# A three-stage hybrid layer: first tiles, router, gathers and weights of each stage fetched and prepared inside the stage before it

## The reference, cut to what matters

```
x = x + attn_a(layernorm(x))     # softmax attention, 16 heads of 64, rotary q and k, full (not causal)
x = x + ffn(layernorm(x))        # one expert of 8 per sequence, chosen from the sequence's last row
x = x + attn_b(layernorm(x))     # causal linear attention in buckets of 64
x = x + ffn(layernorm(x))        # the same weights again

def ffn(h):                      # h: [B, S, 1024]
    last = h[:, -1, :]
    logits = gelu(last @ Wp1 + bp1) @ Wp2 + bp2       # the router, in fp32
    sel = argmax(softmax(logits), -1)
    w1, w2 = W1[sel], W2[sel]                         # [1024, 2048] and [2048, 1024] per sequence
    t = gelu(h @ w1 + b1[sel]) @ w2 + b2[sel]
    return h + 0.3 * (t @ Wo + bo)

def attn_b(h):                   # q, k, v = h @ Wq.T, h @ Wk.T, h @ Wv.T, in 16 heads
    q = softmax(q * 64**-0.25, -1); k = elu(k * 64**-0.25) + 1
    context = cumsum(k.T @ v over buckets) / (cumsum(sum of k) + 1e-6), shifted by one bucket
    return (q @ context) @ Wo.T + bo
```

## Time and profile before

| | |
|---|---|
| median of 3 runs | 3585.08 us |
| the profiled execution | 3589.35 us |
| its span, slowest core (4) | 3587.6 us |
| spans of the eight cores | 3550.1 to 3587.6 us |
| mean granted TensorE clock of the cores | 0.946 to 0.953 |
| TensorE busy | 3156.5 us (88%), 16026 instructions |
| ScalarE, VectorE, POOL busy | 1766.9, 1426.8, 720.7 us |
| chain that ended last, by engine | PE 67%, DVE 8%, ACT 7%, DMA 7%, issue 6%, POOL 4% |

### The profile page before, as it was taken

How to read it: one execution, slowest core, us unless ns; L and a number is a source line. 1 busy time by engine, 2 the same in 40 slices (tenths; PEclk the granted TensorE clock), 3 DMA queues, 4 the chain that set the end, 5 groups by cost and what they waited for, 6 DMA issues and landing times.

```text
span 3587.6 us, 48068 instructions; the slowest of 8 cores (3550.1 to 3587.6 us)
## 1 busy us (share of the span) xinstructions
PE 3156.5 (88%) x16026; PEld 1291.3 (36%) x16026; DVE 1426.8 (40%) x2150; ACT 1766.9 (49%) x2011; POOL 720.7 (20%) x834
## 2 busy tenths in 40 slices
PE   3899999985899999983899899689999946999999
PEld 1332222222332222221344344245545522444444
DVE  3545555543545555432122122156656640232122
ACT  3339999973259999951232223145544422222221
POOL 3410000002310000003321312123322214123311
PEclk9999999997999999995999899899999977999999
DMA  9100000114100001117611421441111129123211
GB/s 169 57 1 1 15 34 25 35 44 119 41 1 1 24 26 35 36 54 146 129 48 48 94 76 43 109 85 60 60 66 64 44 84 158 58 84 70 73 47 48
DMA packets 74892, 216.04 MB, mean 60 GB/s; under 512 B 12128, under 2 KB 14240, under 8 KB 74272
## 3 DMA queue, kind: packets, MB, share of 16 engines
q1 hardware_dynamic: 49728, 157.87, 13.4%
q0 software_dynamic: 24928, 55.11, 9.8%
HBM read 198.80 MB, written 69.21 MB: 75 GB/s over the span
## 4 chain that ended last, share of the span: by engine, by line
PE 67%; DVE 8%; ACT 7%; DMA 7%; issue 6%; POOL 4%; SPq 0%; DVEq 0%; ACTq 0%; POOLq 0%
PE wide L791 12%; PE wide L780 10%; PE bank L683 10%; PE wide L673 6%; PE wide L822 6%; ACT e_sb L1250 6%; PE bank L806 6%; PE bank L910 3%; PE bank L650 3%; PE bank L698 3%; PE bank L689 3%; DMA w2s<-fW,idxw 2%; PE bank L581 2%; PE wide L606 1%; DVE pv_x L1000 1%
## 5 line engine op out<-in xcount | busy, mean ns | idle before, releaser
L1250 ACT ACTIVATE e_sb<-wide 128x1024 bf16<-128x1024 f32 x1024 | 1019.5, 1027 | 86.2 <-PE bank L683 37.4
L683 PE MATMUL bank<-e_sb,v_sb 128*128 128x512 bf16 x2048 | 620.5, 381 | 13.3 <-DVE pv_x L1000 10.1
L780 PE MATMUL wide<-f_xnT,w1s 128*128 128x512 bf16 x2048 | 458.3, 385 | 80.1 <-DMA w1s<-fW,idxw 49.1
L791 PE MATMUL wide<-h_sb,w2s 128*128 128x512 bf16 x2048 | 464.4, 384 | 24.5 <-issue 12.8
L1274 ACT ACTIVATE h_sb<-wide,b1f 128x512 bf16<-128x512 f32 x256 | 175.7, 687 | 550.3 <-PE wide L780 481.9
L673 PE MATMUL wide<-ring,k_sb 64*128 64x512 bf16 x2048 | 401.7, 388 | 16.6 <-ACT e_sb L1250 11.2
L383 POOL TENSOR_TENSOR rt<-raw,cos_t 128x512 bf16<-128x512 bf16 x128 | 147.7, 1154 | 1001.9 <-DVE raw L1038 778.4
L780 PEld LDWEIGHTS wide<-f_xnT,w1s 128*128 128x128 bf16 x2048 | 202.1, 99 | 333.5 <-issue 99.2
L1085 DVE COPY f_xnT<-bank 128x1024 bf16<-128x1024 bf16 x64 | 44.1, 691 | 682.7 <-PE bank L581 682.7
L791 PEld LDWEIGHTS wide<-h_sb,w2s 128*128 128x128 bf16 x2048 | 199.7, 98 | 268.0 <-issue 42.2
L673 PEld LDWEIGHTS wide<-ring,k_sb 64*128 64x128 bf16 x2048 | 103.0, 93 | 443.8 <-issue 443.8
(11 more groups left out here) (175 smaller groups left out, 3559.8 us busy)
## 6 DMA issues: line engine op xcount, KB each, us to landing
a_xt<-xin SPq DMA_DIRECT2D x64, 512.0 KB, 3.8
f_xt<-xs SPq DMA_DIRECT2D x64, 512.0 KB, 4.2
xs<-a_xt SPq DMA_DIRECT2D x32, 512.0 KB, 2.7
xs<-f_xt SPq DMA_DIRECT2D x32, 512.0 KB, 4.9
b_xt<-xs SPq DMA_DIRECT2D x32, 512.0 KB, 3.3
xs<-b_xt SPq DMA_DIRECT2D x32, 512.0 KB, 2.6
yout<-f_xt SPq DMA_DIRECT2D x32, 512.0 KB, 4.5
wof<-fWo POOLq DMA_DIRECT2D x4, 1024.0 KB, 18.4
```

The source lines that it names most:

```text
L683: ins = t.matmul(half[4 + hh], v_sb[:, kc, hp, hh * 64:hh * 64 + 128], e_sb[:, i % 4, hh * 512:(hh + 1) * 512], start=(kc == 0), stop=(kc ...
L780: ins = t.matmul(half[fc % 2], w1s[s][:, c, fc * 128:(fc + 1) * 128], xT[:, c, :], start=(c == 0), stop=(c == NCH - 1))
L791: ins = t.matmul(half[2 + jc % 2], w2s[:, fc, jc * 128:(jc + 1) * 128], h_sb[:, fc, :], start=(fc == 0), stop=(fc == NFC - 1))
L1250: a.activation(e_sb[:, i % 4, :], wide[i % 2][:].rearrange("p a b -> p (a b)"), AF.Exp, scale=INV_SCALE_A).then_inc(sm["ex"], N("ex", (s, i)))
```

## The change: what it does, and the diff

- `all_of` is gone. Engines wait for the single results that they need.
- SBUF is laid out by offsets (`put`), stage by stage, so that what a stage fetches early lies where the stage before has already finished. `w2s` becomes two halves of eight chunks in separate places; it is still one copy of w2.
- Start: four tile buffers (`x_buf`: `a_xt` and `a_xe`) instead of two for sequence 0.
- Sequence 1 of stage 0: tiles 0 to 7 are loaded, normalised on VectorE (`dve_early`) and transposed (`pe_early_flip`) inside the last query group of sequence 0, one in each block. Two V half tiles and the eighth transpose go ahead of sequence 0's last output projection.
- The router runs for one sequence at a time, in four steps (`pe_router`, `dve_router`), each set of inputs loaded again (`load_router`): FFN 1, s = 0 within the K projection of sequence 1; FFN 3, s = 0 within linear attention at j = 19 to 22; s = 1 of both within the first group of the FFN itself, after W2 columns 0, 2, 4 and 6.
- The gathers for FFN 1's first sequence are issued within sequence 1's attention (w1 in two halves, w2's first half; its second half after the last `values`), those of FFN 3's within linear attention (j = 24, 26, 28).
- FFN 1's first four tiles are prepared in the last query group of sequence 1; the last output projection of stage 0 is spread over the hidden columns 4 to 11 of FFN 1. FFN 3's first four tiles pass through linear attention's last iterations, and its first two hidden columns stand before linear attention's last output projection.
- Linear attention's weights and first tiles are loaded within FFN 1's second half, and tile 0 is transposed before its last output projection.

The diff, cut to its core:

```diff
+    def ln_buf(s, t):
+        return t % 4 if s == 0 else 1 if t < 8 else 1 + t % 2
+
+    def o_buf(s, t):
+        return 0 if t < 12 else ((0, 2, 3, 0), (0, 1, 2, 3))[s][t - 12]
...
+            if s == 1:
+                g.wait_ge(sm["rdv"], V("rdv", (1, 0, "idx")))
+                g.wait_ge(sm["vmm"], V("vmm", (s, NG * 8 - 1)))
+                gather_w1(g, 1, 0, range(0, 4))
...
+            else:
+                g.wait_ge(sm["qmm"], V("qmm", (s, "q", NG - 1, NCH - 1)))
+                gather_w1(g, 1, 0, range(4, 8))
+                for k in range(4):
+                    pool_rstd(g, (1, k), k)
+                gather_w2(g, 1, 0, range(0, 8))
...
     def pool_ffn(g, n):
-        all_of(g, n - 1)
...
-        gather(g, n, 0, "w1")
-        gather(g, n, 0, "w2")
-        load_w(g, n, "wo", wof, dr["fWo"])
-        g.wait_ge(sm["gb1"], V("gb1", (n, 0)))
-        gather(g, n, 1, "w1")
+        f = F_[n]
+        if n == 1:
+            g.wait_ge(sm["pv"], V("pv", (1, NG * NCH * NT - 1)))
+            gather_w2(g, n, 0, range(8, NFC))
+            g.wait_ge(sm["om"], V("om", (0, 1, NT - 1, 1)))
+        g.wait_ge(sm["bo3"], V("bo3", n))
+        load_w(g, n, "wo", f.wo, dr["fWo"])
+        pool_router_ones(g, n, 1)
...
+            if G == 0:
+                g.wait_ge(sm["rdv"], V("rdv", (n, 1, "idx")))
+                g.wait_ge(sm["gb1"], V("gb1", (n, 0)))
+                gather_w1(g, n, 1, range(NCH))
+            if G == NG and n == 1:
+                load_w(g, 2, "wq", x_q, dr["bWqT"])
+                load_w(g, 2, "wk", x_k, dr["bWkT"])
+        if n == 1:
+            g.wait_ge(sm["hm"], V("hm", (n, 2 * NG - 1, NFC - 1)))
+            load_w(g, 2, "wv", x_v, dr["bWvT"])
+            load_w(g, 2, "wo", x_o, dr["bWoT"])
...
+            if j == NT + 1:
+                pool_router_ones(g, 3, 0)
+            if j == NT + 8:
+                g.wait_ge(sm["rdv"], V("rdv", (3, 0, "idx")))
+                gather_w1(g, 3, 0, range(0, NCH))
+            if j == NT + 10:
+                gather_w2(g, 3, 0, range(0, 8))
+            if j == NT + 12:
+                gather_w2(g, 3, 0, range(8, NFC))
...
+            for t in range(12):
+                if t > 0:
+                    stored(sy, (0, s, t - 1))
+                elif s == 0:
+                    sy.wait_ge(sm["lna"], V("lna", (n, 0, 12)))
+                load_o(sy, s, t)
+                for r in (2 * (t - 8), 2 * (t - 8) + 1):
+                    if t >= 8 and s == 0:
+                        if r > 0:
+                            sy.wait_ge(sm["lnv"], V("lnv", (n, 1, r - 1)))
+                        else:
+                            sy.wait_ge(sm["lna"], V("lna", (n, 0, 13)))
+                        load_kv(sy, 1, r)
+                    elif t >= 8 and r < 4:
+                        if r > 0:
+                            sy.wait_ge(sm["lnv"], V("lnv", (1, r - 1)))
+                        load_x(sy, 1, (1, "pre", r), "ldp", x_buf[1], 0, r)
+                store_o(sy, s, t)
...
+                load_o(sy, s, 13)
+                load_o(sy, s, 14)
+                stored(sy, (0, s, 11))
+                load_o(sy, s, 12)
+                sy.wait_ge(sm["lnv"], V("lnv", (n, 1, 7)))
+                load_kv(sy, 1, 8)
+                store_o(sy, s, 12)
+                stored(sy, (0, s, 12))
+                load_o(sy, s, 15)
+                store_o(sy, s, 13)
+                stored(sy, (0, s, 13))
+                load_kv(sy, 1, 9)
+                for t in (14, 15):
+                    store_o(sy, s, t)
+                all_stored(sy)
+                sy.wait_ge(sm["nrm"], V("nrm", (s, NG * NCH - 1)))
+                load_router(sy, 1, 0)
+                for t in range(10, NT):
+                    sy.wait_ge(sm["lna"], V("lna", (n, 1, t - 2)))
+                    load_kv(sy, 1, t)
+                sy.wait_ge(sm["lna"], V("lna", (n, 1, NT - 2)))
...
+                stored(sy, (0, s, 11))
+                load_o(sy, s, 12)
+                sy.wait_ge(sm["lnv"], V("lnv", (1, 3)))
+                load_o(sy, s, 13)
+                for k in range(4):
+                    load_x(sy, 1, (1, k), f"ld{k + 4}", F_[1].xt[:, k, :], 0, k)
+                sy.wait_ge(sm["pv"], V("pv", (s, NG * NCH * NT - 1)))
+                load_o(sy, s, 14)
+                load_o(sy, s, 15)
+                for t in range(12, NT):
+                    store_o(sy, s, t)
...
+        if n == 1:
+            sy.wait_ge(sm["nrm"], V("nrm", (1, NG * NCH - 1)))
+        else:
+            sy.wait_ge(sm["lna"], V("lna", (2, NSEQ * NT + 3)))
+        sy.dma_start(f.bo[:], dr["fbo"][0:1, :].partition_broadcast(128)).then_inc(sm["bo3"], N("bo3", n, 16))
...
+        for k in range(0 if n == 3 else 4, 8):
+            load_x(sy, n, (n, k), f_ld(k), f.xt[:, k % 8, :], k // NT, k % NT)
+        load_router(sy, n, 1)
...
+            if k == nk - 5 and n == 1:
+
+                sy.wait_ge(sm["hm"], V("hm", (n, 2 * NG - 1, NFC - 1)))
+                for j in range(2):
+                    load_b(sy, 2, j)
+                sy.wait_ge(sm["rm"], V("rm", (n, 2 * NG - 1, NCH - 1)))
+                for j in range(2, 6):
+                    load_b(sy, 2, j)
...
-        all_of(sy, n - 1)
         all_stored(sy)
         sy.dma_start(bbo_bc[:], dr["bbo"][0:1, :].partition_broadcast(128)).then_inc(sm["bo"], N("bo", n, 16))
...
+            if k == NT:
+                stored(sy, (n, NT - 1))
+                load_router(sy, 3, 0)
...
+    def pe_early_flip(t, sem_key):
+
+        t.wait_ge(sm["lnv"], V("lnv", sem_key))
+        pe_flip(t, a_xn[:], 6, "tr", sem_key)
...
+    def pe_router(t, n, s, step, bk):
+
+        r = R_[n, s]
+        if step == 0:
+            t.wait_ge(sm["xl"], V("xl", (n, s)))
+            t.wait_ge(sm["rpl"], V("rpl", (n, s, "ones")))
+            ins = t.matmul(half[bk][:, 0:8], r.ones[:], r.xl[:], start=True, stop=True)
...
+        else:
+            for hh in range(2):
+                t.wait_ge(sm["nev"], V("nev", (0, NG * NCH - 1, hh)))
+                pe_v(t, n, s, vo[hh], None)
+            pe_early_flip(t, (n, 1, 7))
+            t.wait_ge(sm["trd"], V("trd", (n, 1, 7)))
+            for u in range(8):
+                pe_last_out(t, n, 0, u)
...
+                ahead = (g_ + 1) * 4 if s == 0 else 8 + g_ * 4
+                if ahead < NT and c >= 4:
+                    pe_a_flip(t, n, s, ahead + c - 4)
+                if s == 1 and (g_, c) in ((1, 3), (2, 0), (2, 5), (3, 4)):
+                    if g_ == 1:
+                        t.wait_ge(sm["vev"], V("vev", (s, 12)))
+                    pe_router(t, 1, 0, ((1, 3), (2, 0), (2, 5), (3, 4)).index((g_, c)), 4)
...
+            if kc == 4 and qg == NG - 1 and r > 0:
+                if r > 1 and (s == 0 or r < 5):
+                    t.wait_ge(sm["trd"], V("trd", (n, 1, r - 2) if s == 0 else (1, r - 2)))
+                else:
+                    t.wait_ge(sm["rope"], V("rope", ((s, "q", NG - 1, NCH - 1), "t2")))
+                if s == 0 or r < 5:
+                    pe_early_flip(t, (n, 1, r - 1) if s == 0 else (1, r - 1))
```

```diff
+    def pe_ffn(t, n, done):
...
+            for fc in range(done if G == 0 else 0, NFC):
+                pe_hidden(t, n, G, fc)
+                if G == 0 and n == 1 and 4 <= fc < 12:
+                    pe_last_out(t, 0, 1, fc - 4)
...
+                if G == 0 and jc % 2 == 0:
+                    pe_router(t, n, 1, jc // 2, 4)
...
+                if j - NT in (3, 4, 5, 6):
+                    i = j - NT - 3
+                    pe_router(t, 3, 0, i, 6)
+                    if i == 2:
+                        t.wait_ge(sm["rac"], V("rac", (3, 0)))
+                    else:
+                        t.wait_ge(sm["rdv"], V("rdv", (3, 0, ("sq", "var", "", "lg")[i])))
                 proj(j, x_k, "wk", 6, "bk_")
...
+            if j == nj:
+                for fc in range(2):
+                    pe_hidden(t, 3, 0, fc)
```

VectorE's side of the early tiles, and its first wait in linear attention:

```diff
+    def dve_early(v, key, k, prev, ld, ldkey):
+
+        dve_stats(v, key, k, x_buf[1], ld, ldkey)
+        if prev:
+            v.wait_ge(sm["tr"], V("tr", prev))
+        v.wait_ge(sm["lnr"], V("lnr", key))
+        v.tensor_scalar(a_xn[:], x_buf[1], rn[:, k % 8, 0:1], rn[:, k % 8, 1:2], ALU.mult, ALU.add
+                        ).then_inc(sm["lnv"], N("lnv", key))
+
+    def dve_early_out(v, key, dst):
+        v.wait_ge(sm["tr"], V("tr", key))
+        v.tensor_copy(dst, flip(6)).then_inc(sm["trd"], N("trd", key))
+
...
-            dve_stats(v, n, j, b_xt, 6)
+        v.wait_ge(sm["bo"], V("bo", n))
```

859 lines of the change are left out of this document (483 added, 376 removed).

## The result

The changed kernel takes 3415.69 us (median of 4 runs, 3411.16 to 3686.69) against 3584.9 us before. The three others lie at 3411.16, 3412.46 and 3418.92, and their ratio to before is 0.9522 (95% interval 0.9503 to 0.9541). The forecast was 3349 us with a range up to 3402: the kernel is faster, as forecast, but 62 us or more slower than forecast.

The account below looks back on a forecast made before the run. TensorE's steady work plus five stage starts set the time. Terms -13 - 38 + 2 - 93.5 - 45.3 + 29 - 77 = -235.8 from 3589.35 give 3353.5, median 4.3 lower: 3349; own range 3325 to 3375, wider 3312 to 3402.

Parts of the forecast that it names:

- TensorE should not see them: Linear attention: nine gathers, 11 us on POOL, fit between two POOL products 17.5 apart, costing TensorE nothing.
- Attention to FFN 1: Last value product to FFN 1: -108.8 up to the first W2 product, +5.3 router products, +10 wait and clock: -93.5.
- They land some 16 us after the last output product: FFN 1's router inputs: TensorE wants them at +10.4, so waits 5.3, raised to 8; bounds nothing and 25.
- FFN 1 to linear attention: Start of linear attention, 62.6 us, shrinks to 17.3, with the bias late behind residual and store (3.8): -45.3.
- Linear attention to FFN 3: Start of FFN 3: -86.6 up to the W2 products, +5.3 router products, +4 their wait and clock: -77.
- Eight tiles ahead of it nearly fit: FFN 3's router inputs: TensorE arrives at +27.7, so it waits only some 2 us for them.
- Linear attention: Inside the stage: four router steps delay K by some 7.3 us each with the low clock: +29, bounds 0 and 45.
- The score and value loops: Attention blocks: the early tiles cost TensorE 11 transposes of 0.45 us, partly in existing room: +2.
- rival B: Attention: early tiles delay VectorE, each of 11 blocks overruns by 3 us and restarts at low clock: +55, 3404; chance 0.17.
- Rival A: Linear attention, attention and FFN: router waits cost almost nothing, 29 and 10 us less: about 3310; chance 0.14.
- D: Whole kernel: a semaphore chain holds gathers or tiles at the old place, time stays at 3585; chance 0.02.
- Rival C: Between the five starts: granted clock falls in dense stretches; 3660 if 10% of matmul work is affected; chance 0.05.

Follow-up runs that it names:

- r2: Changed kernel with the 2 MB of FFN output weights started only after the router's inputs have landed: 3386.02 and 3423.82 us.
- r11: Changed kernel with the same 2 MB of FFN output weights loaded a second time behind the first: ratio 0.963 to the kernel before the change.
- r3: Changed kernel with linear attention's 2 MB of output weights issued only after the bias has landed: 3404 to 3428 us, ratio 0.9506 to the kernel before the change.
- r4: Changed kernel with linear attention's four router products moved ahead of Q, in the transposes' bank: ratio 0.9452 to the kernel before the change.
- r6: On top of r4, gathers spread: at most four in an iteration of linear attention, and spread out in attention too: 3367.03 and 3369.93 us.
- r7: Changed kernel with FFN 1's W1 and first W2 gathers issued only after attention's last value product: ratio 0.9645 to the kernel before the change.
- r10: Changed kernel with r1, r3, r4, r6, r8 and later FFN router products together: median 3329.39 us, ratio 0.9282 to the kernel before the change.
- r8: On top of r3, linear attention's bias issued before its first tiles, and engines wait for single stores: ratio 0.9464 to the kernel before the change.
- r1: Changed kernel with the FFN router's five inputs issued ahead of bias and tiles on SyncE: ratio 0.9481 to the kernel before the change.

## Why the prediction was wrong

**What failed** are two steps, each with about half of the 58.9 us: the price of landings, where a transfer moved into a busy stretch was to land as it did in another one (some 30 us in three terms), and "TensorE should not see them", of the gathers (some 28 in two).

- Attention to FFN 1 (-93.5 forecast, -78.1 measured). "They land some 16 us after the last output product" failed. The last output product ended at 1577.2, the last input landed at 1609.5, 32 us later, and the router ran at 1609.9; TensorE wanted it at 1587.5, as forecast. I took 11.9 us from the earlier trace rows for the landing, but that is the median of eight tiles, and the inputs stand behind the last of them: without the weights the wait is still 11.4 (r2), not 5.3. For the 2 MB of weights I added 3; r2 shows that they cost 11, r11 that 2 MB more cost 14. The rule cited there (the Trainium skill, DMA: Bandwidth & Descriptors, "Issuing engines are not separate DMA queues") holds, and r2 shows it; the prediction gave it a price of 3 us, where it was the main term. The two landing times that the prediction set beside the rule could not test it, since the 11.9 had SyncE's own eight tiles and GpSimd's gathers in one window. Its -108.8 for the first part came out as -104.1.
- FFN 1 to linear attention (-45.3, measured -34.6). The mechanism, the bias behind the last store, was right. "Residual and store 3.8" was 15.9: the store's 2.7 of the earlier trace rows is a median over the whole span, this store had 4 MB of weights beside it. r3 gives back 10.6 us for 2 MB.
- Linear attention to FFN 3 (-77, measured -66.5). "Eight tiles ahead of it nearly fit", a wait of 2, was 10.9; the weights beside them were not counted. r2 brings it to nothing on core 0.
- Linear attention (+29, measured +46.1). The router steps were right to the microsecond (29.3), and r4 shows it. What failed is "TensorE should not see them", of POOL's gathers: 17.1 us on core 0, 2 us or less on the other die. It was argued from GpSimd's time alone. TensorE's waits behind the bursts name ScalarE and VectorE, on one die, and cost it 12 to 18 us by r4 and r6, up to 38 in r3; the slowest core of the profiled execution is on that die.
- The score and value loops (+2, measured +13.0). The forecast's rival B had the place and the mechanism in part. On core 0 VectorE waited for an early tile behind the gathers at 1411 us and TensorE 4.08 us for its evicted copy, in one block and not in eleven. r6 and r7 take 6.5 us (mean) away, and r6 leaves 553.9 to 554.4 us on every core, 1.3 to 1.8 over core 4 before: the early tiles' +2 was right, and the 11 us over it on core 0 were the gathers. The forecast had no term for them here.
- Start and first junction came out better than forecast by 1.3 and 4.5 us; no run took them apart.

Two of these stand at the upper bounds that the prediction itself gave: the wait at FFN 1's router (22.4 of 25) and linear attention (46.1, bound 45). Its range to 3402 left room for 53 us in all, too little for several at once.

**What was right:** the direction, the 29 us of linear attention's router steps, and that what is late next at the three later junctions is the router's inputs and the bias. Rival A (more hidden than seen) and D are out. Rival C (the clock falls in dense stretches) is not seen in the profiled execution: its clock rose from 0.947 to 0.972 and 0.976, and to 0.984 in r10. The 1.95 GHz for sustained work that the prediction quotes from the Trainium skill (TensorE: Matmul & The Clock Gate, "Seeing it yourself") would be a granted clock of 0.81; no profiled execution here shows it as a mean.

**What stays open:** why ScalarE and VectorE of one die start late beside a burst of gathers, when no engine of their own core held them back ("remote" in the trace), and why it is one die in each run and not always the same. That spreading takes most of it away is shown; the path is not. Why two cores lose twice as much in r3, r7 and r8 is open as well. The share of tiles against router in the 65 us of the first large term is open too.

## What to carry to other kernels

Price a transfer that you move by the bytes that all queues will have ahead of it at its new place, and not by its landing time at the old one; here some 200 GB/s explained what 2 MB of weights cost within 4 us (10.6, 11 and 14 us in r3, r2 and r11). For a transfer behind others a median landing is too low, since it is that of the middle one. The small inputs on which a decision hangs go first, and bulk weights that are wanted 50 us later wait for them. Then look at the order on each engine: an operation behind an unrelated wait (the fill behind the bias, the bias behind the last store) keeps the stall alive when the bytes are gone. A serial chain of small steps belongs where the answering engine idles, in a bank that nobody needs, and gathers go out a few at a time. The last helps the slowest core; measure what it costs in the stages behind.

## What the runs showed of the hardware that was not expected

- An issue can block: SyncE stood 17.61 and 22.49 us in issuing 0.5 KB with four and eight tiles of its own ahead and GpSimd's 2 MB of weights beside them. Without the weights, and with the same queue of its own, it was 7.40 and 9.57 us (r2); with only the router's first two inputs ahead 2.29 (r1).
- 2 MB of weights on GpSimd's queue delayed SyncE's inputs by 11 us (r2), 2 MB more by 14 (r11), also where SyncE had no more than 2.5 MB ahead of them itself. In FFN 1 2.10 MB of them took as much of the DMA engines' time as 3.06 MB of SyncE's (48.1% and 47.7%).
- Bursts of 8 or 9 gathers held up ScalarE and VectorE by some 5 us on all four cores of one die and on none of the other, in r3 VectorE by some 11 us on two cores; at most four at a time left 1.4 to 3.3 us in one iteration (r6).
